# A cross-attention and expert kernel: one ReLU moved from ScalarE to VectorE, and share matmuls over 64 rows

## The reference

```python
probs = softmax(xn @ Wr + br)                  # 8 experts
scores, idx = top_k(probs, 2)
full[e] = relu(xn @ W1[e] + b1[e]) @ W2[e] + b2[e]      # F = 512
c[e]    = relu(b1[e]) @ W2[e] + b2[e]
output  = sum over the 2 chosen e of scores * (full[e] - c[e] + c_total)
```

## Time and profile before

| | us |
|---|---|
| three runs | 3741.14, 3741.39, 3743.73 |
| median | 3741.39 |
| the profiled execution's own time | 3743.73 |
| its span, first to last instruction | 3742.0 |
| PE busy | 3642.2 |
| ACT busy | 2606.0 |
| DVE busy | 1763.7 |
| POOL busy | 448.3 |

### The profile page before, as it was taken

One profiled execution on the slowest core, in us unless ns is written; L12 is line 12 of the kernel. 1 busy time (PEld: TensorE's weight loads), 2 busy tenths in 40 slices (PEclk: granted clock), 3 DMA queues, 4 the chain that ended last, 5 costly groups with the idle time before them and its releaser, 6 DMA issues.

```text
span 3742.0 us, 83174 instructions
## 1 busy us (share of the span) xinstructions
PE 3642.2 (97%) x32098; PEld 1365.7 (36%) x32102; DVE 1763.7 (47%) x1873; ACT 2606.0 (70%) x2701; POOL 448.3 (12%) x1721
## 2 busy tenths in 40 slices
PE   8999999999999999999999999999999999999999
PEld 4333333334433333333333333343222223344444
DVE  3222222224377777777777777763321220223445
ACT  6999999993455555555556555559999999732342
POOL 2222222220000000000000000013322332200000
PEclk9999999999999999999999999999999999999999
DMA  6323232212111111111111110000000000011000
GB/s 198 101 70 107 84 103 81 98 70 68 66 39 40 39 39 41 39 35 39 40 39 40 39 40 17 1 24 5 4 4 4 4 30 2 13 29 42 0 1 6
DMA packets 99788, 163.04 MB, mean 44 GB/s; under 512 B 22404, under 2 KB 39200, under 8 KB 97920
## 3 DMA queue, kind: packets, MB, share of 16 engines
q1 hardware_dynamic: 99456, 158.16, 13.2%
HBM read 93.24 MB, written 64.88 MB: 42 GB/s over the span
## 4 chain that ended last, share of the span: by engine, by line
PE 80%; ACT 12%; issue 5%; DVE 2%; ACTq 0%; DMA 0%; SPq 0%; POOL 0%; DVEq 0%; POOLq 0%
PE ps L1027 18%; PE ps L1052 18%; PE ps L701 11%; ACT probs L1455 7%; PE ps L633 4%; ACT probs L1466 4%; PE ps L523 3%; PE ps L898 3%; PE ps L529 3%; PE ps L916 3%; PE ps L1226 2%; PE ps L1221 2%; PE ps L663 1%; PE ps L1331 1%; PE ps L1348 1%
## 5 line engine op out<-in xcount | busy, mean ns | idle before, releaser
L1622 ACT ACTIVATE probs<-ps 128x1024 f32<-128x1024 f32 x808 | 828.2, 1025 | 588.5 <-PE ps L1027 576.3
L1466 ACT ACTIVATE probs<-ps 128x1024 f32<-128x1024 f32 x1200 | 1119.3, 1031 | 49.8 <-PE ps L633 34.1
L2558 DVE TENSOR_TENSOR vbuf<-vbuf,probs 128x1024 f32<-128x1024 f32 x784 | 953.4, 1224 | 331.4 <-ACT probs L1622 331.4
L701 PE MATMUL ps<-probs,vst 128*32 128x512 f32 x6400 | 844.6, 599 | 27.2 <-ACT probs L1466 24.1
L2284 DVE COPY qs<-ps 128x512 f32<-128x512 f32 (+1 forms) x208 | 141.6, 681 | 564.9 <-PE ps L529 282.8
L1455 ACT ACTIVATE probs<-ps 128x1536 f32<-128x1536 f32 x268 | 362.1, 1624 | 3.4 <-PE ps L681 1.8
L1798 POOL CAST kst<-kb 128x128 fp32r<-128x128 f32 (+1 forms) x800 | 250.1, 313 | 743.3 <-PE ps L701 595.3
L1027 PE MATMUL ps<-probs,kb 64*64 64x512 f32 x2560 | 332.2, 589 | 0.0
L1052 PE MATMUL ps<-probs,qz 64*64 64x512 f32 x2048 | 267.2, 592 | 1.8 <-DVE kb L2583 1.8
L1052 PE MATMUL ps<-probs,kb 64*64 64x512 f32 x2048 | 265.7, 589 | 0.0
L1027 PE MATMUL ps<-probs,qz 64*64 64x512 f32 x1856 | 243.2, 595 | 3.1 <-DVE cols L1996 2.8
(11 more groups left out here) (453 smaller groups left out, 3682.4 us busy)
## 6 DMA issues: line engine op xcount, KB each, us to landing
kv_scratch<-qs SPq DMA_DIRECT2D x192, 256.0 KB, 2.0
kb<-kv_scratch SPq DMA_DIRECT2D x72, 256.0 KB, 2.9
qz<-kv_scratch SPq DMA_DIRECT2D x56, 256.0 KB, 2.9
kb<-k_scratch SPq DMA_DIRECT2D x12, 816.0 KB, 7.0
vbuf<-in_L_ffn_W SPq DMA_DIRECT2D x32, 256.0 KB, 3.1
klo<-kv_scratch SPq DMA_DIRECT2D x32, 256.0 KB, 2.9
qs<-kv_scratch SPq DMA_DIRECT2D x32, 256.0 KB, 2.9
qz<-q_scratch SPq DMA_DIRECT2D x56, 64.0 KB, 2.1
```

Source lines behind the costliest of these rows:

```text
L701: mm = pe.matmul(ps[band, 6 + half, :], vst[:, r, band], probs[:, r, j * HT:(j + 1) * HT], start=start, stop=stop)
L1466: act.activation(probs[:, r, b * T:(b + 1) * T].rearrange("p (h n) -> p h n", h=2), ps[:, 2 * buf:2 * buf + 2, :], ACT.Exp, scale=HD8 ** - ...
L1622: act.activation(pr1[:, (u + (u == LAST1) + 2 * odd) % 4], ps[:, 2 * b:2 * b + 2, :], ACT.Exp, scale=HD64 ** -0.5)\
L2558: dve.tensor_tensor(sum1[:, odd, h], sum1[:, odd, h], e, ALU.add).then_inc(s["added"], 1)
```

## The change

1. In `experts8(1)` the four evictions with ReLU of each expert go from ACT to DVE. DVE computes `max(h + (b1 - relu(b1)), -relu(b1))`, which is `relu(h + b1) - relu(b1)`, from two new rows of `rb1`. So the output comes without c[e], and the copy and subtraction of L924's column go from the combination; the L924 matmuls stay, since their sum is needed at the end.
2. DVE's `shares8(1)` comes behind the first expert's evictions. Two operations over 128 x 32 are added ahead of `layernorm(6)`.
3. The share matmuls of all three expert layers read 64 rows in place of 128. POOL no longer clears `shares`; in `experts8` the 0/1 column is a new tile `pick` that POOL copies anew for each expert (`weights8`), two columns used by turns, and PE waits for it (`ccol_ready`).
4. ACT's load of the square root table stands ahead of `experts8(1)` instead of behind it.

```diff
-        rb1 = sb("rb1", [P, 2, E8 * NF])
+        rb1 = sb("rb1", [P, 3, E8 * NF])
+        pick = sb("pick", [P, 2], F32R)
-        shares = qz[:, 0:2 * HT].rearrange("p (h n) -> p h n", h=2)
+        shares = qz[0:64, 0:2 * HT].rearrange("p (h n) -> p h n", h=2)
...
                 def weight8(n, u, h):                                        # PE
+                    pe.wait_ge(s["ccol_ready"], n + 1)
                     pe.wait_ge(s["cb_copied"], n * 2 + h + 1)
-                    pe.matmul(ps[:, 6, :], picked[:, n % E8:n % E8 + 1].to_broadcast([P, P]), shares[:, h, :],
+                    pe.matmul(ps[:, 6, :], pick[0:64, u:u + 1].to_broadcast([64, P]), shares[:, h, :],
...
-                pe.matmul(ps[:, 6, :], picked[:, n - 1:n].to_broadcast([P, P]), shares[:, q, :],
+                pe.matmul(ps[:, 6, :], picked[0:64, n - 1:n].to_broadcast([64, P]), shares[:, q, :],
...
-            load_table(5, ACT.Relu)                                          # ACT
+            load_table(5, ACT.Sqrt)
             experts8(1)
-            load_table(5, ACT.Sqrt)
...
-            def shares_cleared(m):                                           # POOL
-                pool.wait_ge(s["exp_done"], UNITS[2 * m + 1] + RING)
-                pool.memset(shares.bitcast(F32), 0.0).then_inc(s["ccol_ready"], 1)
+            def weights8(m):
+                pool.wait_ge(s["comb_ready"], m + 1)
+                with pool.Fori(0, E8 // 2) as i:
+                    for u in range(2):
+                        n = i * 2 + u + E8 * m
+                        pool.wait_ge(s["eo_ready"], n + 1)
+                        pool.tensor_copy(pick[:, u:u + 1], picks[:, bass.ds(i * 2 + u, 1)]).then_inc(s["ccol_ready"], 1)
...
-                        if m == 1 and e == 0:                                # DVE
-                            shares8(1)
+                        if m == 1:
+                            for f in range(NF):
+                                dve.wait_ge(s["h_ready"], n * NF + f + 1)
+                                if f == 0:
+                                    dve.wait_ge(s["eo_ready"], n + 2)
+                                dve.tensor_scalar(hid[:, f, :, :], ps[:, 2 * (f % 2):2 * (f % 2) + 2, :],
+                                                  rb1[:, 1, e * NF + f:e * NF + f + 1], rb1[:, 2, e * NF + f:e * NF + f + 1],
+                                                  ALU.add, ALU.max).then_inc(s["hid_ready"], 1)
+                            if e == 0:
+                                shares8(1)
...
-                            then(dve.tensor_copy(rb1[:, 1, e:e + 1], ps[:, 7, e:e + 1]))
-                            dve.scalar_tensor_tensor(out=t1, in0=ps[:, 4:6, :], scalar=rb1[:, 1, e:e + 1], in1=t3,
-                                                     op0=ALU.subtract, op1=ALU.mult).then_inc(s["eo_used"], 1)
+                            dve.tensor_tensor(t1, ps[:, 4:6, :], t3, ALU.mult).then_inc(s["eo_used"], 1)
...
             then(dve.tensor_scalar(rb1[:, 0, :], b1c[:, 1, :], 0.0, None, ALU.max))
+            dve.tensor_tensor(rb1[:, 1, :], b1c[:, 1, :], rb1[:, 0, :], ALU.subtract)
+            then(dve.tensor_scalar(rb1[:, 2, :], rb1[:, 0, :], -1.0, None, ALU.mult))
```

More of the change, by code:

```diff
@@ L89 @@
 NIDENT = 2
-NCONST = 28
+NCONST = 27
 ADDED = {1: 0, 3: H * ST}
@@ L1551, in experts8 @@
                         for f in range(NF):
[L1552 to L1556, removed]
+                            if m == 0:
+                                act.wait_ge(s["h_ready"], n * NF + f + 1)
+                                if f == 0:
+                                    act.wait_ge(s["eo_ready"], n + 2)
+                                act.activation(hid[:, f, :, :], ps[:, 2 * (f % 2):2 * (f % 2) + 2, :], ACT.Gelu,
+                                               bias=b1c[:, 0, bass.ds(e * NF + f, 1)]).then_inc(s["hid_ready"], 1)
                         for h in range(2):
@@ L1755, in _ @@
                 diagonal(picks[:, :], [[-1, E16]], -32 * j)
-            const(pool.memset(picked[:, :].bitcast(F32), 0.0))
-            const(pool.tensor_copy(picked[0:64, :], picks[0:64, :]))
+            const(pool.tensor_copy(picked[:, :], picks[:, :]))
             const(pool.memset(ctxT[C:P, ONES:S], 1.0))
@@ L1888, in stage2 @@
                             stage_values(t - 1, (t - 1) % RING, g)
-            def shares_cleared(m):
-                pool.wait_ge(s["exp_done"], UNITS[2 * m + 1] + RING)
-                pool.memset(shares.bitcast(F32), 0.0).then_inc(s["ccol_ready"], 1)
+            def weights8(m):
[5 more added lines that the diff above has]
+                        pool.tensor_copy(pick[:, u:u + 1], picks[:, bass.ds(i * 2 + u, 1)]).then_inc(s["ccol_ready"], 1)
             stage0()
-            shares_cleared(0)
+            weights8(0)
             for p in range(NP):
@@ L1905, in _ @@
             stage2()
-            shares_cleared(1)
+            weights8(1)
             mode3 = mode_of(pool, 3)
@@ L2354, in shares8 @@
                 dve.wait_ge(s["turned"], 4 + m)
-                dve.wait_ge(s["ccol_ready"], m + 1)
                 dve.tensor_copy(shares[0:E8], ps[0:E8, 6:8, :]).then_inc(s["w_copied"], 1)
@@ L2366, in experts8 @@
                         n = e + E8 * m
-                        if m == 1 and e == 0:
-                            shares8(1)
+                        if m == 1:
+                            for f in range(NF):
+                                dve.wait_ge(s["h_ready"], n * NF + f + 1)
+                                if f == 0:
+                                    dve.wait_ge(s["eo_ready"], n + 2)
[4 more added lines that the diff above has]
+                                shares8(1)
                         dve.wait_ge(s["moe_acc"], n + 1)
```

## The result

The changed kernel takes 3777.9 us (median of 4 runs, 3776.16 to 3778.97), the kernel before 3741.3 (4 runs beside it, 3740.73 to 3743.73): the ratio is 1.0095, with a 95% interval of 1.008 to 1.0111. That is 36.6 us slower, by the interval 30 to 42. The forecast was 3779, within 3764 to 3794.

What follows compares the result with a forecast made beforehand. PE was taken as the bound, busy 3642.2 of 3742.0 us. Terms 5.6 + 5.1 + 0.4 - 0.2 + 25 + 1.5 = 37.4 us on the median 3741.4 gave 3779 us, 8-in-10 range 3764 to 3794.

Steps and rivals of the forecast that it cites:

- share matmuls: All three expert layers: 64-row matmuls between 128-row neighbours empty PE, +0.42 us each, +25 us in all.
- later experts: Second expert layer: first eviction stands behind the previous expert's combination on DVE; PE loses 0.8 us each, 5.6 for seven.
- clock: PE's idle time in the first expert brings a half-clock stretch: 1.5 us taken, bounds 0 to 3.4.
- first expert, gap: Second expert layer: first eviction stands behind DVE's routing, so PE's third block loads 5.1 us later.
- two small operations: Two DVE operations added before `layernorm(6)`, hidden by nothing: +0.4 us.
- last combination: DVE's shorter combination behind the eighth expert, on the chain to the next layernorm: -0.2 us.
- seven behind one-column matmuls: Share matmuls whose load was exposed before already: 0.8 us taken off the share matmul cost.
- A: Rival: no emptying between 64 x 128 and 128 x 128 share matmul shapes; +12.4, 3754 us; chance 0.12.
- B: Rival: share matmuls run beside their neighbours, saving 0.24 each, 15.4 in all; 3738 us; chance 0.03.
- C: Rival: both loads behind a share matmul exposed, 0.6 each, 11.5 us more; 3790 us; chance 0.07.

Runs made afterwards that it cites:

- ReLU alone: The kernel before with only the ReLU evictions' move to DVE and its accompanying edits, share matmuls kept at 128 rows: 3754.85 against 3742.3 us, ratio 1.0032.
- 64 rows alone: The kernel before with only the 64 share matmuls of all three expert layers reading 64 rows: 3765.0 against 3742.3 us, ratio 1.006.

## Why the prediction was right

Every step has the sign and place forecast; the sum, 37.4, is 36.6 by the medians. That it is so close is in part luck: the share matmuls (2.5) and the later experts (0.7) were put too high, and the clock too low. Term by term, forecast and found:

| term | forecast | found | from |
|---|---|---|---|
| first expert, gap | 5.1 | 5.2 | both profiles, first load to third block |
| seven later experts | 5.6 | 4.9 | ReLU alone, 0.7 each |
| two small operations | 0.4 | 0.3 | offsets +0.33 and +0.31 at the second layernorm |
| last combination | -0.2 | -0.2 | DVE's chain behind the last product, 2.52 against 2.77 |
| share matmuls | 25 | 22.5 | 6.2 + 5.5 + 10.9 |
| clock | 1.5 | 2.9 | 6.59 against 3.70 |
| sum | 37.4 | 35.6 | |

*Later experts.* The eviction is longer than forecast (1.34 recorded, not 1.28), the stall still shorter. DVE's instructions overlap: in the rows after, L2377 starts 0.09 before L2392's recorded end, and from DVE's first instruction to PE's load are 3.79 us where I had added up 3.87. The lower bound of the forecast, 0.55, was worked out from just this; I chose the sum of durations and should have gone halfway.

*Share matmuls.* The mechanism and the signs (late load, exposed load behind it, 3.2 us per step) came out as written, the size was 0.03 too large: the wait behind the stream is 0.09, not the 0.12 read from the earlier trace rows, which are of other pairs of shapes. 64 x 0.03 = 1.9. The seven behind one-column matmuls are cheaper as said: 5.5 in the second layer against 6.2 in the first with as many matmuls. The last layer absorbs 1.2 in three steps (1 forecast).

*Clock.* One stretch of 5.6 us on the path, not one of 3.4 half on it. The term was within its bounds (0 to 3.4) and larger than taken. That the pause brings such a stretch, which the term rests on, held in one of two profiles: with the ReLU alone the same pause was followed by full clock. The profile of before had more half clock around the first expert layer (0.83 against 0.91 between 870 and 890 us), which takes 1.6 us off the difference of the spans: the first expert layer grew by 4.6 us there and not by the forecast's 6.7, where 64 rows alone, at the clock of before, added 6.2. Without the clock the found terms give 32.7, so by the medians 3.9 are left for the clock and for what no run isolates; the interval of the whole, 30 to 42, can't tell that from the 1.5 forecast.

*Rivals.* A (no emptying) would have been 3754; the rows alone moved 22.7. B (not slower) fell with it. C (0.6 per matmul) isn't seen: the two loads behind a share matmul take 0.30 together, as after any hole, and the step is 3.20, not 3.4.

## What to carry to other kernels

Before halving the rows of a small matmul, look at its neighbours: one matmul of 64 rows between matmuls of 128 costs 0.39 us here, more than its whole step of 0.24; 96 rows cost nothing that can be measured (ratio 0.9999), and a pair of 64-row matmuls in a row pays once. When work moves to an engine that takes its instructions in order, look at what stands ahead of it there and not only at its duration: the evictions of the same seven experts cost 4.9 us behind a two-step combination, and nothing when the first two of each expert stood between its steps. An engine that is half idle over the whole kernel (DVE, 47%) can be full in the stretch that counts (4.36 of 4.80 us).

## What was not expected of the hardware

A matmul over 96 rows is recorded as 96*128 and is treated like one of 128: load pulled ahead, 2.81 us per step as before. The record's shape is thus the tile's, and doesn't tell by itself whether the array changes its shape; the idle time ahead of the load (0.76 against 0.24) does.

An FP32 TENSOR_SCALAR from PSUM with two scalars per partition took 1.34 us for 128 x 1024 (the one of the earlier trace rows 1.28); two in a row took 2.59 to 2.60, the second starting 1.26 behind the first, before its recorded end.

A pause of PE was followed by half clock in one profile and not in another of the same shape: 3.47 us idle and then 5.6 us at 0.50 in the changed kernel, 3.46 idle and then 1.00 with the ReLU alone.
